# Attention followed by a bidirectional mixer on one core: the maxima turned inside the step, scores a place further ahead, and predicated copies and a moved residual in the mixer

## The reference

```python
x = x + attention(layernorm(x))   # 32 query heads of 32, one key/value head, causal, 512 tokens
x = x + ffn(layernorm(x))         # one 1024 x 1024 product plus a low-rank update
x = x + mixer(layernorm(x))       # down to 128, gelu, two bidirectional scans ("hydra"), up to 1024
x = x + ffn(layernorm(x))

def mixer(u):                     # u is also the residual inside: x_init
    h = xmid = gelu(u @ w_down.T + b_down)
    h = hydra(hydra(h))           # conv of 7 taps, forward and backward scan, gate, norm
    h = xmid + alpha * xmid + (1 - alpha) * h
    return u + h @ w_up.T + b_up
```

## Time and profile before

| | |
|---|---|
| three runs | 2946.77, 2938.45, 2946.47 us; median 2946.47 us |
| profiled execution | 2937.39 us, its span 2935.6 us |
| mean granted clock of TensorE | 0.967 of full speed |
| PE busy | 2706.6 us (92%) |
| DVE busy | 1676.3 us (57%) |
| ACT busy | 1151.1 us (39%) |
| POOL busy | 947.0 us (32%) |

### The profile page before, as it was taken

One profiled execution on the slowest core, in us unless ns is written; L12 is line 12 of the kernel. 1 busy time (PEld: TensorE's weight loads), 2 busy tenths in 40 slices (PEclk: granted clock), 3 DMA queues, 4 the chain that ended last, 5 costly groups with the idle time before them and its releaser, 6 DMA issues. The chain is left out here.

```text
span 2935.6 us, 41188 instructions
## 1 busy us (share of the span) xinstructions
PE 2706.6 (92%) x14784; PEld 1961.1 (67%) x14784; DVE 1676.3 (57%) x4305; ACT 1151.1 (39%) x2509; POOL 947.0 (32%) x1460
## 2 busy tenths in 40 slices
PE   5888999999999999999999987999999999999988
PEld 3555666657566676575665566777777777777766
DVE  3563564663745646636444346666666666666653
ACT  3763464562644645626455013222222222222220
POOL 2333122221231122212313044444444444444412
PEclk8999999999999999999999888999999999999989
DMA  5764554454536455544455410010101010101001
GB/s 159 209 169 151 176 125 143 126 115 145 126 91 172 124 140 130 113 150 120 107 146 172 145 43 1 7 52 7 52 6 53 6 53 5 54 5 54 5 26 29
DMA packets 103628, 272.24 MB, mean 93 GB/s; under 512 B 12122, under 2 KB 23514, under 8 KB 101122
## 3 DMA queue, kind: packets, MB, share of 16 engines
q1 hardware_dynamic: 102706, 269.55, 34.0%
q10 hardware_dynamic: 720, 0.07, 0.0%
HBM read 168.40 MB, written 50.33 MB: 75 GB/s over the span
## 5 line engine op out<-in xcount | busy, mean ns | idle before, releaser
L668 DVE CUSTOM_DVE_ANT_0 ps_attn<-ps_attn,later_keys 128x512 f32<-128x512 f32 (+3 forms) x1024 | 488.1, 508 | 392.8 <-PE ps_attn L841 392.3
L474 POOL TENSOR_SCALAR_AFFINE_SELECT pt<-pt 128x512 f32<-128x512 f32 x256 | 163.4, 649 | 868.1 <-ACT pt L561 868.1
L1564 PE MATMUL ps_mixer<-m_w_hi,m_xt_hi 128*128 128x512 f32 x1024 | 418.2, 408 | 1.6 <-DVE m_xt_lo L1346 1.6
L561 ACT ACTIVATE pt<-ps_attn 128x512 f32<-128x512 f32 (+1 forms) x704 | 380.4, 558 | 82.8 <-PE ps_attn L868 75.8
L1566 PE MATMUL ps_mixer<-m_w_lo,m_xt_hi 128*128 128x512 f32 x1024 | 400.6, 391 | 0.0
L1565 PE MATMUL ps_mixer<-m_w_hi,m_xt_lo 128*128 128x512 f32 x1024 | 400.4, 391 | 0.0
L576 ACT ACTIVATE ps_attn<-ps_attn,top 128x512 f32<-128x512 f32 (+1 forms) x512 | 311.6, 609 | 214.7 <-DVE top L668 214.0
L841 PE MATMUL ps_attn<-k_stack,q_stack 96*128 96x512 f32 (+3 forms) x1024 | 304.0, 348 | 42.8 <-ACT ps_attn L576 17.5
L868 PE MATMUL ps_attn<-q_stack,k_stack 97*128 97x512 f32 (+1 forms) x704 | 298.1, 426 | 30.3 <-DMA q_stack<-top_rows 18.9
L1246 ACT CAST m_xt_hi<-ps_mixer 128x512 fp32r<-128x512 f32 x192 | 103.6, 589 | 506.0 <-PE ps_mixer L1559 505.7
L841 PEld LDWEIGHTS ps_attn<-k_stack,q_stack 96*128 96x128 f32 x1024 | 182.8, 194 | 105.4 <-ACT ps_attn L576 64.6
(11 more groups left out here) (216 smaller groups left out, 4915.7 us busy)
## 6 DMA issues: line engine op xcount, KB each, us to landing
xr<-in_a_x SPq DMA_DIRECT2D x64, 512.0 KB, 6.6
q_stack<-q_hi SPq DMA_DIRECT2D x128, 256.0 KB, 5.6
wq_hi<-wq_split SPq DMA_DIRECT2D x56, 512.0 KB, 3.9
wq_lo<-wq_split SPq DMA_DIRECT2D x56, 512.0 KB, 4.9
q_stack<-q_lo SPq DMA_DIRECT2D x64, 256.0 KB, 6.8
wo_hi<-wo_split SPq DMA_DIRECT2D x8, 2048.0 KB, 8.1
wo_lo<-wo_split SPq DMA_DIRECT2D x8, 2048.0 KB, 13.3
x<-xr SPq DMA_DIRECT2D x32, 512.0 KB, 2.8
```

The costliest lines, as they stand in the source:

```text
L561: nc.scalar.activation(pt[k][:, heads[0]:heads[0] + len(heads), :].rearrange("p j t -> p (j t)"), ps[:, ST0 + n % 2, 0:width * len(heads)] ...
L668: mm = nc.vector.tensor_tensor_reduce(part, part, later_keys[:, T - width:T], 1.0, NO_SCORE, ALU.add, ALU.min, top[:, j * TILES + i:j * TI ...
L1564: nc.tensor.matmul(out, a_hi, b_hi, start=first, stop=False)
```

## The change

In the attention:
- `tops_turned`, `copy_rows` and `shift` of group M+1 move from the start of step M+1 into step M, ahead of its last turned unit, except for groups 6 and 7 of a batch that has a next one (`turned_early`).
- Chunks 0 and 1 of the query product of group M+3 are done in step M, behind turned units 8 and 9, where `begun_early` allows it: groups 5, 6, 7, 1 and 2 of a batch. The other six chunks stand later in step M+1 than before.
- Scores run a unit further ahead of the turned units; `weigh_first` follows the second score unit.
- `q_high` stands one unit later on ACT, `q_low` one on DVE, and `finish_high` always at the end of a step.

In the mixer:
- The addition of the normed input to the residual of kind 2 leaves POOL. One ACT instruction for each tile (`add_normed`) multiplies the stream by 1 + inv_std and adds -mean * inv_std, in place; three short POOL instructions make the two factors.
- `cb` is set to the identity once, in `small_params`; `h_weight` then writes the two sides over it by predicated copies. `cb_fw` and its memset go.

The two conditions:

```diff
+        def turned_early(G):
+            return inside(G) and not (G % GROUPS >= GROUPS - 2 and G // GROUPS + 1 < BATCH)
+        def begun_early(G):
+            M = G - 3
+            return (M >= 0 and inside(G) and output_run(M) is None and coming(M + 1, 6) is None and coming(M, 5) is None)
```

SP, at the start of a step and behind the loads of its middle:

```diff
-                    if inside(M):
+                    if inside(M) and not turned_early(M):
                         shift(M)
...
+                    if turned_early(M + 1):
+                        shift(M + 1)
                     if (run := output_run(M)) is not None:
```

ACT:

```diff
                     for u in range(U):
+                        if u == U - 1 and turned_early(M + 1):
+                            copy_rows(M + 1)
                         if inside(M):
                             exps(M, (u,))
                         if inside(M + 1):
                             row_sum(M + 1, u + 2)
-                        if u == (2 if second is not None else 1) and inside(M + 2) and M != -1:
+                        if u == (4 if second is not None else 2) and inside(M + 2) and M != -1:
                             q_high(M + 2)
```

DVE:

```diff
-                        tops(M + 1, (4, 5) if second is not None else (4,))
-                    if inside(M + 2) and M != -1:
+                        tops(M + 1, (4, 5))
+                    if second is None and inside(M + 2) and M != -1:
                         q_low(M + 2)
```

PE:

```diff
-                    shares = ((0, 1, 2, 3, 4), (5, 6), (7,), (), (), ()) if M == -1 else ((0,), (1,), (2,), (3, 4), (5, 6, 7), ())
+                    if M == -1:
+                        shares = ((0, 1, 2, 3, 4), (5, 6), (7,), (), (), ())
+                    elif begun_early(M + 2):
+                        shares = ((), (2,), (), (3, 4), (5, 6), (7,))
+                    else:
+                        shares = ((), (0,), (), (1, 2), (3, 4), (5, 6, 7))
                     if project:
                         q_part(M + 2, shares[0])
-                    if inside(M):
+                    if inside(M) and not turned_early(M):
                         tops_turned(M)
...
                     for u in range(U):
+                        if u >= U - 2 and begun_early(M + 3):
+                            q_part(M + 3, (u - U + 2,))
+                        if u == U - 1 and turned_early(M + 1):
+                            tops_turned(M + 1)
                         if inside(M):
                             turned_scores(M, u)
-                        if u + 2 < U and inside(M + 1):
-                            scores(M + 1, u + 2)
+                        if inside(M + 1):
+                            for n in ((2, 3), (4,), (5,), (6,), (7,), (8,), (9,), (10,))[u] if u < 8 else ():
+                                scores(M + 1, n)
```

The mixer, `post` on POOL:

```diff
-                    pool.wait_ge(xn_done, e + 1)
                     if kind == 2:
-                        for cols in pieces:
-                            nc.gpsimd.tensor_tensor(stream[:, cols], stream[:, cols], xn[:, e % 2, cols], ALU.add).then_inc(up_bias, 1)
-                        pool.wait_ge(up_bias, PIECES * (kind2.index(e) + 1))
+                        pool.wait_ge(res_done, kind2.index(e) + 1)
```

ACT, called behind `x_high` of an event of kind 2:

```diff
+                def add_normed(e):
+                    n, stream = kind2.index(e), stream_of(e)
+                    act.wait_ge(xn_done, e + 1)
+                    act.wait_ge(res_scale, 3 * (n + 1))
+                    nc.scalar.activation(stream, stream, ACT.Identity, bias=res_shift[:, n % 2:n % 2 + 1],
+                                         scale=res_gain[:, n % 2:n % 2 + 1]).then_inc(res_done, 1)
```

`h_weight` on DVE, where the last four of the five old instructions are left out:

```diff
-                    nc.vector.tensor_tensor(cb_fw[:, :, PB:P], cb_ps[:, :, 0:cut],
...
+                    nc.vector.copy_predicated(cb[:, :, PB:P], con["before"][:, None, PB:P].to_broadcast([P, TILES, cut]).bitcast(U32),
+                                              cb_ps[:, :, 0:cut]).then_inc(cb_done, 1)
+                    dve.wait_ge(cb_done, 2 * q + 1)
+                    nc.vector.copy_predicated(cb[:, :, 0:cut], con["after"][:, None, 0:cut].to_broadcast([P, TILES, cut]).bitcast(U32),
+                                              cb_ps[:, :, PB:P]).then_inc(cb_done, 1)
```

More of the change, by code:

```diff
@@ L14 @@
 U8 = mybir.dt.uint8
+U32 = mybir.dt.uint32
 PENDING = []
@@ L644, in _ @@
                             x_high(first, 1)
-                    if output_run(M) is not None or M == STEPS[-1]:
-                        for G in finishes(M):
-                            finish_high(G)
+                    for G in finishes(M):
+                        finish_high(G)
             @block.vector
@@ L737, in _ @@
                     if inside(M + 1):
-                        tops(M + 1, (4, 5) if second is not None else (4,))
-                    if inside(M + 2) and M != -1:
+                        tops(M + 1, (4, 5))
+                    if second is None and inside(M + 2) and M != -1:
                         q_low(M + 2)
                     if inside(M + 1):
-                        tops(M + 1, (6, 7) if second is not None else (5, 6, 7))
+                        tops(M + 1, (6, 7))
+                    if second is not None and inside(M + 2):
+                        q_low(M + 2)
                     if inside(M - 1):
@@ L855, in tops_turned @@
                         pe.wait_ge(top_rows_done, G)
-                    if b and g in (1, 2):
-                        pe.wait_ge(y_added, Y_TILES * (b - 1) + TILES * g)
+                    if b and g in (2, 3):
+                        pe.wait_ge(y_added, Y_TILES * (b - 1) + TILES * (g - 1))
                     nc.tensor.transpose(ps[:, MISC, 0:P], top[:, :].bitcast(F32), ident_f).then_inc(topt_ready, 1)
@@ L916, in output @@
                         else:
-                            pe.wait_ge(top_rows_done, min(GROUPS * (b + 1) + run + 1, NG))
+                            pe.wait_ge(top_rows_done, min(GROUPS * (b + 1) + run + 2, NG))
                         tok = slice(t * P, (t + 1) * P)
@@ L943, in _ @@
                         scores(M + 1, 1)
+                    if inside(M - 1):
+                        weigh_first(M - 1)
                     if project:
@@ L1225, in _ @@
                 nc.gpsimd.memset(neg_half[:, :], -0.5).then_inc(setup, 1)
-                nc.gpsimd.memset(cb_fw[:, :, :], 0.0).then_inc(setup, 1)
                 nc.gpsimd.memset(ones[:, :], 1.0).then_inc(setup, 1)
-                pool.wait_ge(setup, 3)
+                pool.wait_ge(setup, 2)
                 for name, i, what, *part in plan:
@@ L1499, in small_params @@
                                                 ALU.mult).then_inc(small, 1)
+                    nc.vector.tensor_copy(cb[:, :, :], con["ident"][:, None, :].to_broadcast([P, TILES, P])).then_inc(small, 1)
                 def weight_low(n):
```

48 lines of the change are left out of this document (25 added, 23 removed).

## The result

| | before | after |
|---|---|---|
| median of nine runs | 2946.47 us (2938.45 to 2951.97) | 2959.41 us (2938.61 to 2970.14) |
| ratio | | 1.0046, 95% interval 1.0024 to 1.0068 |
| profiled execution's span | 2935.6 us | 2957.7 us |

The account below looks back on a forecast made before the run. It took the query chain, as late as the maxima, to bound ordinary attention steps. Attention +17 and mixer -19 gave -2 us; between two bases it predicted 2940 us, no change, range 2895 to 2965 (the forecast's own 2931 to 2949).

Parts of the forecast that it names:

- The query chain: Attention, ordinary step: 9.20 us from last query matmul to next score unit, 7.74 back; as late as the maxima.
- Steps 3 and 4: Attention steps preparing groups 5 and 6 of a batch: +0.1 us each, bounds 0 and +1.2.
- step 7: Attention step preparing group 1 of the next batch: q_high later on ScalarE, +0.3 us, bounds 0 and +1.2.
- step 2: Attention step preparing group 4: all eight query chunks and three more units lie inside the chain, +1.4 us.
- The signs that the prediction named: First score unit waits for q_lo; early transposition waits over 1 us in steps 0 and 1; mixer waits shrink or vanish.
- Steps 0 and 1: Attention, before output products: early transposition waits about 1.2 us; step 0 loses two chunks, -0.5; step 1 +0.6.
- Steps 5 and 6: Attention: step 5 loses two query chunks, half kept, -0.7 us; step 6 has two more, less a wait, +1.2.
- Batch 0: First batch of the attention: waits for loads, set at nothing, +-4 us.
- The mixer: Residual off GpSimd -9.6 us, mixing matrices by predicated copies -7.3, waits at start and last block -2.8; sum -19.
- The shift as a rival: Steady attention: shift lands 0.9 us too late for the first turned unit in 28 steps, +25, 2965 us; chance 0.2.
- the 17 of the sum: Attention, seven batches after the first at +2.5 us each: +17 us.
- The bound of +45 for the attention: Upper bound of the attention's loss, if q_high costs its 1.2 us in full in four steps of seven batches.

Follow-up runs that it names:

- q_high_later: Attention of before with the change's mixer, plus only the later q_high and q_low in step 6; 2902.1 us, 0.9867 of the kernel before.
- scores_back: The changed kernel with the scores no further ahead of the turned units than before; 2928.3 us, 0.9950 of the kernel before.
- ahead_alone: Attention of before with the change's mixer, plus scores a unit further ahead and the later q_high and q_low in step 6; 3040.2 us, ratio to before 1.0325.
- shift_first: The changed kernel with SP issuing the shift ahead of the output weights' store and load; 2937.5 us, 0.9979 of the kernel before.

## Why the prediction was wrong

- **What bounds, right.** The query chain ends last in steps 2, 3, 4 and 7, as read: 7.70 and 9.50 us in the step shown. Steps 3 and 4 of batches 1 to 7 changed by -0.1 in the mean (+0.1 forecast), step 7 by +0.3 (+0.3), step 2 by +1.3 (+1.4). The signs that the prediction named came too: the waits for q_lo, the early transposition's wait of 1.0, the two waits of the mixer gone or at most 0.6.
- **Steps 0 and 1, half right.** The transposition waits 1.0 us (1.2 forecast) in front of the output product; that the granted clock may fall behind it was not in the sum. In all seven batches step 1 lost 7.3 where 4.2 were forecast, step 0 lost 2.2 where 3.5 were to be won. Without the five falls, 1.6 each, step 1 would have lost 4.1 and step 0 won 2.6 (an estimate from their lengths).
- **Steps 5 and 6, right as a sum only.** +3.2 and -0.4 over the batches against -4.9 and +7 to 8. Two effects were missed that nearly cancel: q_high's later place in step 6 gives 2.5 us a step (q_high_later), and the scores' reach takes them away (step 6 of scores_back is 2.2 shorter than the change's). That the sum came out near was luck.
- **Batch 0, the step that failed:** "Batch 0 waits for loads and is set at nothing (+-4)". It lost 16.7. The loads did not hide the change: the scores' reach costs 15 us there (ahead_alone 195.2 against 180.2; scores_back undoes 16.2). The units that the reach moved were priced by their 0.23 us on TensorE, and not by the row sum that each must wait for. The shift, which I took as issued earlier, stood on SP behind the wait for GpSimd as it had before; shift_first shows a gain that was missed there (25.1), and not a second part of the 16.7.
- **The mixer, right term by term:** -9.4 of L1559's waits for -9.6, -7.3 for -7.3, the first and last waits -1.3 each for -1.4, 20 in all for 19 (its three terms add to 19.7).
- **The shift as a rival** did not come in the steady attention: the turned units' wait for top_rows is 0.7. The Trainium skill's rule on the semaphore, that its increment lands only after every earlier write of that DMA engine ("DMA: Bandwidth & Descriptors", "Queues, rings and completion order"), agrees with the trace of the changed kernel: in none of the 64 groups did the shift land ahead of the queries issued before it, and in step 1 of batches 1 to 7 its landing took 6.0 to 8.1 us (1.8 in the median of all), 0.2 to 1.2 behind theirs. No turned unit waited for it there, behind the output product, so it cost nothing. The late shift of batch 0 was late by its place in SP's program.

Without batch 0's 16.7 the measured +13 would have been -4; the batches after it lost 23 for the 17 of the sum. The bound of +45 for the attention held (+42).

## What to carry to other kernels

A unit that is issued further ahead is not free because its engine has room: ask which buffer it writes, who must release that, and what stands behind it on its in-order queue. Look for the reverse too, an instruction that stands in its queue ahead of what it waits for, as q_high did in step 6: the idle time in front of it is on an engine that looks unimportant. And price the stage that "waits for something else" like any other, with the queue that its transfers stand in.

## What the runs showed of the hardware

In step 0 of batch 6 TensorE's granted clock, after a wait of 1.03 us, was 0.72 of full speed over a window of four microseconds and 1.00 again in the next; in the same place of another batch, with the same wait, it stayed at 1.00, as these windows of step 0 of batch 7 show.

```profile
1477.00:1481.00 4.00, 2.97 (x20) 1.99 (x20) 2.80 (x16) 2.74 (x6) 1.76 (x3) 1.00 0.50 59
1481.00:1485.00 4.00, 4.00 (x19) 3.29 (x18) 0.00 (x0) 0.00 (x0) 4.00 (x4) 1.00 0.01 2
```

What decides between the two was not found. A predicated copy of 448 columns from PSUM takes 0.65 us, 7% more than the product of the same size.
